# Token attention of a decoder: Q and K projections as three products of split fp32r parts, weights split step by step, and the last unit of each batch summed by VectorE alone

## The reference, cut to what matters

```python
def _attn_block(q_src, k_src, v_src, Wq, Wk, Wv, Wo, bo):
    q = _split_heads(q_src @ Wq)
    k = _split_heads(k_src @ Wk)
    v = _split_heads(v_src @ Wv)
    dots = jnp.einsum('bhid,bhjd->bhij', q, k) * SCALE
    attn = jax.nn.softmax(dots, axis=-1)
    out = jnp.einsum('bhij,bhjd->bhid', attn, v)
    ...
    return out @ Wo + bo
out = x1 + _attn_block(x1, x2, x2, Wq, Wk, Wv, Wo, bo)
return _attn_block(out, out, x1, Wq, Wk, Wv, Wo, bo)
```

## Time and profile before

| what | value |
|---|---|
| median of 3 runs | 2540.93 us (2538.76 to 2542.99) |
| the profiled execution's own time | 2538.74 us, its span 2537.0 us |
| a unit in the middle of stage c | 22.4 to 22.6 us |
| mean granted TensorE clock | 0.955 of 2.4 GHz |
| busy over the span | PE 91%, DVE 58%, ACT 43%, POOL 43% |
| stage b | about 502 to 721 us |
| stage c | about 721 to 1644 us: batch 0 to 1151, batch 1 after it |

### The profile page before, as it was taken

How to read it: one execution, slowest core, us unless ns; L and a number is a source line. 1 busy time by engine, 2 the same in 40 slices (tenths; PEclk the granted TensorE clock), 3 DMA queues, 4 the chain that set the end, 5 groups by cost and what they waited for, 6 DMA issues and landing times.

```text
span 2537.0 us, 34125 instructions
## 1 busy us (share of the span) xinstructions
PE 2317.5 (91%) x12790; PEld 1410.6 (56%) x12790; DVE 1466.7 (58%) x2191; ACT 1089.5 (43%) x2285; POOL 1091.9 (43%) x795
## 2 busy tenths in 40 slices
PE   6989999879988999998999998699899589979998
PEld 3333443357744444444544443488656466768887
DVE  6778678357735666662666663342443656655556
ACT  1667567623323444441344444042321457743223
POOL 2556546424443788875577888133400122100000
PEclk7899989989999999999999999799999799989999
DMA  6445333222110111011001111056210051010001
GB/s 128 119 89 96 76 57 71 68 79 37 1 1 1 14 14 14 10 14 5 5 10 14 14 14 14 7 133 173 32 73 18 34 131 56 1 50 26 1 1 34
DMA packets 136594, 110.29 MB, mean 43 GB/s; under 512 B 74759, under 2 KB 114165, under 8 KB 136429
## 3 DMA queue, kind: packets, MB, share of 16 engines
q1 hardware_dynamic: 99277, 107.16, 15.8%
q0 software_dynamic: 36864, 0.15, 4.2%
q10 hardware_dynamic: 288, 0.79, 0.2%
HBM read 83.11 MB, written 12.35 MB: 38 GB/s over the span
## 4 chain that ended last, share of the span: by engine, by line
PE 78%; DVE 10%; ACT 4%; POOL 2%; DMA 2%; issue 2%; SPq 2%; ACTq 0%; DVEq 0%; POOLq 0%
PE PS L115 74%; SPq L141 2%; POOL c_AC L119 2%; DVE g_SS L119 1%; PE PS L1181 1%; ACT a_P L834 1%; DVE a_MX L728 1%; PE PS L347 1%; DVE g_st L1266 1%; DMA a_KS<-a_KL 1%; PE PS L348 1%; DVE c_MX L1707 1%; DVE X L391 0%; ACT g_SS L1338 0%; POOL adj L340 0%
## 5 line engine op out<-in xcount | busy, mean ns | idle before, releaser
L340 POOL DMA_INDIRECT adj<-e_EE,e_IX x256 | 412.8, 1612 | 459.3 <-DMA adj<-e_EE,e_IX 344.6
L119 POOL TENSOR_TENSOR c_AC<-c_AC,c_P 128x1024 f32<-128x1024 f32 x160 | 401.3, 2508 | 98.9 <-DVE c_AC L119 91.4
L1707 DVE TENSOR_REDUCE c_MX<-PS 128x2 f32<-128x1024 f32 x256 | 312.8, 1222 | 193.6 <-PE PS L115 192.6
L1793 ACT ACTIVATE c_P<-PS 128x1024 f32<-128x1024 f32 x256 | 249.8, 1023 | 226.2 <-PE PS L115 218.1
L728 DVE TENSOR_REDUCE a_MX<-PS 128x2 f32<-128x1024 f32 x256 | 303.5, 1220 | 58.0 <-PE PS L115 56.4
L834 ACT ACTIVATE a_P<-PS 128x512 f32<-128x512 f32 x512 | 270.7, 602 | 89.5 <-PE PS L115 84.9
L115 PE MATMUL PS<-c_P,c_VV 128*64 128x512 f32 x1024 | 249.2, 608 | 0.0
L124 POOL TENSOR_SCALAR e_EQ<-e_KR,e_KC 128x128 bf16<-128x128 f32 x256 | 162.4, 634 | 160.3 <-DMA e_KR<-adj_key 122.1
L115 PE MATMUL PS<-a_QS,a_KS 64*128 64x512 f32 x512 | 195.5, 464 | 20.7 <-ACT a_P L834 8.6
L115 PE MATMUL PS<-a_KS,a_QS 48*128 48x512 f32 x512 | 171.7, 476 | 10.3 <-DVE a_MX L728 5.0
L115 PEld LDWEIGHTS PS<-a_QS,a_KS 64*128 64x128 f32 x512 | 84.5, 190 | 173.6 <-ACT a_P L834 96.3
(11 more groups left out here) (491 smaller groups left out, 4506.5 us busy)
## 6 DMA issues: line engine op xcount, KB each, us to landing
e_KR<-adj_key SPq DMA_DIRECT2D x64, 256.0 KB, 3.4
f_W<-in_L_ffn_w SPq DMA_DIRECT2D x16, 1024.0 KB, 6.3
c_RB<-c_r SPq DMA_DIRECT2D x60, 128.0 KB
g_FB<-in_fside_1x16xSxS SPq DMA_DIRECT2D x8, 616.0 KB, 8.0
a_QS<-a_QH SPq DMA_DIRECT2D x32, 128.0 KB
adj<-e_zt SPq DMA_DIRECT2D x16, 256.0 KB, 4.3
adj<-e_EE,e_IX POOLq DMA_INDIRECT x256, 3.1
d_AJ<-adj SPq DMA_DIRECT2D x8, 512.0 KB, 5.1
```

What stands on the lines that cost most here:

```text
L119: return v.e.tensor_tensor(o, a, b, op)
L340: g.e.indirect_dma_start(self.adj, bass.IndirectOffsetOnAxis(ap=self.IXE[:, k:k + 1], axis=0), self.EE[:, k:k + 1], None, compute_op=ALU.a ...
L1707: v.e.reduce_max(MX[:, w % 2, :, qt, kh], bank(0, 2).rearrange("p (h n) -> p h n", h=2), AX, negate=True).then_inc(*smax_dve.up())
L1793: s.e.activation(PB[t % NP][:, :, :].rearrange("p h n -> p (h n)"), bank(2 + 2 * (t % 2), 2), ACT.Exp, scale=0.125).then_inc(*st_act.up())
```

## The change

1. At the end of stage b each tile is split as it is turned: ACT writes the coarse fp32r part over XT (c_XH), DVE writes the rest (c_XF). The rest of batch 0 lies over b_WO, that of batch 1 over c_OT, from where it goes to DRAM (c_fine); `xt` jobs begin at step 6 instead of 3, since b_WO is in use until then. b_YY has 8 buffers.
2. The weights of a pair are split into c_WS just before their use: `coarse` (two ACT casts of 128x128) and `fine` (two DVE subtractions of 128x128, both inputs in SBUF), once for Wk and once for Wq. In units with odd w up to 27, except 15, they stand at n = 3 to 6. Pairs 0, 1 and 9 are split ahead of the loops.
3. A projection is six fp32r matmuls. In pair 0 the two Q projections use bank 6.
4. In units 15 and 31 DVE does all seven `add`, and POOL does no `acc`.
5. Three 1 MB loads in stage c (`fetch`): the rest of batch 1 for pair 8 (at w = 13, n = 6) and for the later pairs, and Wo again (w = 15, n = 6).
6. `out` of a batch's first four tiles waits for 15 scaled units of it, not 16.

```diff
+    def over(self, name, first, skip, shape, dt=F32R):
+
+        return self.nc.alloc_sbuf_tensor_at(name, shape, dt, offset=self.places[first] + skip)
 
 
 def mm(pe, o, l, r, first=True, last=True):
...
@@ -1056,6 +1061,8 @@
                 for q in range(4):
                     yield "u", 0, q
             if first:
+                if 6 <= i < 9:
+                    yield "xt", 2 * i - 12
                 if 1 <= i < 17:
                     yield "turn", i - 1
                 if i < 16:
@@ -1076,8 +1083,9 @@
                     yield "root", (i - 5) // 4
                 if 5 < i < 20 and i % 4 == 2:
                     yield "norm", (i - 6) // 4
-            if i >= lag:
-                yield "xt", i - lag
+
+            if i >= (6 if first else lag):
+                yield "xt", 2 * i - 11 if first and i < 9 else i - lag
 
     jobs = list(schedule())
     nth = numbered(jobs)
...
                     ins = v.e.bn_aggr(st8[:, i % 8, 6:8], st8[:, i % 8, 0:6])
                     if i % 4 == 3:
                         ins.then_inc(*var_dve.up())
+            elif kind == "xt" and first:
+                i, = a
+                cols = slice(128 * i, 128 * i + 128)
+                v.wait_ge(xt_act, i + 1)
+                v.wait_ge(u_pe, 8)
+                tt(v, K.fine[i // 8][:, :, 128 * (i % 8):128 * (i % 8) + 128], halves(bank(7)[:, 0:256]),
+                   K.coarse[:, :, cols].bitcast(F32), ALU.subtract).then_inc(*xl_dve.up())
             elif kind == "norm":
                 q, = a
                 four = slice(4 * (q % 2), 4 * (q % 2) + 4)
...
             elif kind == "xt":
                 i, = a
                 s.wait_ge(xt_pe, i + 1)
-                s.e.copy(XT[:, :, i * 128:i * 128 + 128], halves(bank(7)[:, 0:256])).then_inc(*xt_act.up())
+                s.e.copy((K.coarse if first else XT)[:, :, i * 128:i * 128 + 128],
+                         halves(bank(7)[:, 0:256])).then_inc(*xt_act.up())
             elif kind == "root":
                 q, = a
...
@@ -1404,7 +1420,10 @@
                     dma(sp, UO[0:80, b, 9, :], udram[b, 1152:1232, :]).then_inc(*u_in[b].up())
                     if not (first or b):
                         bias(*range(2, 8))
-        if not first:
+        if first:
+            sp.wait_ge(xl_dve, 16)
+            dma(sp, K.fdram, K.fine[1][:, :, :]).then_inc(*K.fine_out.up())
+        else:
             K.experts.load_router(sp, A)
             for e in range(2):
                 K.experts.load(sp, A, e)
...
     MT = sb(c, "c_MT", [8, 2, 128], F32R)
+
+    split_w = K.over("c_WS", "LS", 0, [128, 2, 2, 2, 128])
+    WS = [[split_w[:, w, part, :, :] for part in range(2)] for w in range(2)]
+    XH = [K.coarse[:, k, :] for k in range(2)]
+
+
+    WOF, WVF = K.fine[0][:, :, :], K.over("c_WVF", "b_WV", 0, [128, 2, 1024])[:, :, :]
     mdram = K.nc.dram_tensor("c_m", [2, 8, 128], F32R, kind="Internal").ap()
     sdram = K.nc.dram_tensor("c_s", [2, 512], F32, kind="Internal").ap()
     rdram = K.nc.dram_tensor("c_r", [128, 8], F32, kind="Internal").ap()
...
@@ -1461,7 +1488,17 @@
 
         return w % 16 == 15
 
+    def lead(w):
+
+        return 7 if direct(w) else 2
+
+    def leads(w):
+        return sum(map(lead, range(w)))
+
     def schedule():
+        for w in (1, 0):
+            yield "coarse", 0, w
+            yield "fine", 0, w
         yield "prep_k", 0, 0
         yield "prep_q", 0
         yield "prep_k", 0, 1
@@ -1478,6 +1515,11 @@
                     yield "s", 0, kt
                     if kt >= 4:
                         yield "s", 1, kt - 4
+            for w in (1, 0):
+                yield "coarse", 8 * b + 1, w
+                yield "fine", 8 * b + 1, w
+            if b:
+                yield "fetch", 2
             if b == 0:
                 yield "row", 0
                 yield "m", 0
...
                         yield "m", w + 1
-                    if n in (3, 4):
+                    if 3 <= n < lead(w) + 3:
                         yield "add", w, n - 3
-                    if n > 3:
+                    if n - 1 > lead(w):
                         yield "acc", w, n - 1
                     if n == 0 and not first:
                         yield "acc", w - 1, 7
@@ -1507,6 +1549,10 @@
                         yield "recip", w - 2
                     if n == 4 and not first and w - 2 >= 16 * b:
                         yield "scale", w - 2
+                    if w % 2 and w % 16 != 15 and w // 2 + 2 < 16 and 2 < n < 7:
+                        yield ("coarse", "fine")[(n - 3) % 2], w // 2 + 2, n < 5
+                    if n == 6 and w in (13, 15):
+                        yield "fetch", w // 14
                     if n % 2 == 0:
                         continue
...
@@ -1532,7 +1578,8 @@
                     if n in (1, 3, 5):
                         yield "send", 1
             w = 16 * b + 15
-            yield "acc", w, 7
+            yield "add", w, 5
+            yield "add", w, 6
             yield "pv", w, 6
             yield "turn_ou", w
             yield "recip", w - 1
@@ -1565,7 +1612,7 @@
     def added(t):
 
         w, n = divmod(t, 8)
-        return (acc_dve, 2 * w + max(n, 1)) if n < 3 else (acc_pool, 5 * w + n - 2)
+        return (acc_dve, leads(w) + max(n, 1)) if n <= lead(w) else (acc_pool, 7 * w - leads(w) + n - lead(w))
 
     def tensor(_):
...
                 pe.wait_ge(*free[bk])
+
+        def product(w, P, bk, src):
+
+            b = P // 8
+            pe.wait_ge(ws_dve, 2 * P + 2 - w)
+            if b:
+                pe.wait_ge(fine_in, 2 if P > 8 else 1)
+            fine = WVF if P > 8 else WOF
+            high, low = WS[w]
+            parts = [(W, part, k) for k in range(2) for W, part in (
+                (high, XH[k][:, src]), (low, XH[k][:, src]), (high, fine[:, k, src.start - 1024 * b:src.stop - 1024 * b]))]
+            for q, (W, part, k) in enumerate(parts):
+                ins = mm(pe, bank(bk), W[:, k, :], part, q == 0, q == 5)
+            return ins
...
                 t, = a
                 bk = 2 + t % 4
-                pe.wait_ge(ot_pool, 16 * (t // 8 + 1))
+                pe.wait_ge(ot_pool, 16 * (t // 8) + 15 + t % 8 // 4)
+                pe.wait_ge(wo_in, 1)
                 bank_free(bk)
                 for p in range(8):
                     ins = mm(pe, bank(bk)[:, 0:256], OT[:, p, t % 8 * 128:t % 8 * 128 + 128], W0.WO[:, p, :], p == 0, p == 7)
...
             kind, *a = job
-            if kind == "prep_k":
+            if kind == "fine":
+                P, w = a
+                v.wait_ge(ws_act, 2 * P + 2 - w)
+                for k in range(2):
+                    ins = tt(v, WS[w][1][:, k, :], weight(w, P, k), WS[w][0][:, k, :].bitcast(F32), ALU.subtract)
+                ins.then_inc(*ws_dve.up())
+            elif kind == "prep_k":
                 P, half = a
                 cols = slice(half * 512, half * 512 + 512)
...
                 v.wait_ge(qh_act, w + 1)
-                tt(v, QL[w % 3][:, :], bank(7), QH[w % 3][:, :].bitcast(F32), ALU.subtract).then_inc(*ql_dve.up())
+                tt(v, QL[w % 3][:, :], bank(prep_bank(w // 2, False)), QH[w % 3][:, :].bitcast(F32), ALU.subtract).then_inc(*ql_dve.up())
             elif kind == "s":
...
                 t = 8 * w + more
                 v.wait_ge(st_act, t + 2)
                 if more:
-                    v.wait_ge(acc_dve, 2 * w + 1)
+                    v.wait_ge(acc_dve, leads(w) + more)
                 elif w > 1:
                     v.wait_ge(sum_pe, w - 1)
...
             kind, *a = job
-            if kind == "prep_k":
+            if kind == "coarse":
+                P, w = a
+                if P and w:
+                    s.wait_ge(k_pe, 2 * P)
+                elif P:
+                    s.wait_ge(q_pe, 2 * P)
+                if P % 8 == 1:
+                    s.wait_ge(v_pe, 16 * (P // 8 + 1))
+                for k in range(2):
+                    ins = s.e.copy(WS[w][0][:, k, :], weight(w, P, k))
+                ins.then_inc(*ws_act.up())
+            elif kind == "prep_k":
...
@@ -1875,6 +1964,18 @@
                     dma(sp, MR[w % 3][64 * h:64 * h + 1, :],
                         mdram[w % 2][4 * h:4 * h + 4, :].rearrange("j q -> (j q)").rearrange("(o n) -> o n", o=1)).then_inc(
                         *m_in[w % 2].up())
+            elif kind == "fetch":
+                n, = a
+                if n == 1:
+                    sp.wait_ge(q_pe, 18)
+                    dma(sp, W0.WO, A["L0_xattn_Wo"].rearrange("(c p) n -> p c n", p=128)).then_inc(*wo_in.up())
+                else:
+                    sp.wait_ge(K.fine_out, 1)
+                    if n:
+                        sp.wait_ge(v_pe, 32)
+                    else:
+                        sp.wait_ge(q_pe, 16)
+                    dma(sp, WVF if n else WOF, K.fdram).then_inc(*fine_in.up())
             elif kind == "spread":
                 w, = a
...
             ectx.close()
```

(16 more changed lines are left out.)

50 lines of the change are left out of this document (27 added, 23 removed).

## The result

The median of 5 runs is 2517.56 us (2515.36 to 2521.82), against 2538.76 us (2534.32 to 2542.99) for the kernel before on the same chip: a ratio of 0.9921, 95% interval 0.9906 to 0.9936. That is 21 us faster; forecast were 36.6 us. The time is inside the range of 2484 to 2524 us and outside the narrower one, 2495 to 2512, that the forecast had for its own mechanism. The profiled execution has a span of 2515.8 us, 21.2 less than the 2537.0 of before.

The account below looks back on a forecast made before the run. PE was taken to bound stage b and mid stage c, with waits on POOL at batch ends. Terms -33.0 - 3.0 - 3.1 - 13.6 + 0.5 + 15.6 = -36.6 us gave 2502.1 us profiled, 2504 median, range 2484 to 2524.

Parts of the forecast that it names:

- Projections in the loops: Stage c loops: 60 projections fall from 1.92 to 1.37 us of PE each, 33.0 us saved (bounds 24 to 33).
- Collisions: Odd units: the second weight-subtraction pair waits for POOL's acc, PE loses 1.2 us in 13 units, +15.6 us.
- if collisions fell elsewhere than at n = 6: Odd units: one of the signs that the prediction is wrong; no size given.
- End of batch 0: Last unit of batch 0: DVE's adds let sum start earlier, 3.1 us saved (bounds 4.3 and 0).
- End of batch 1: Unit 31: sum no longer waits for POOL, output starts at 1581.0 instead of 1594.62, 13.6 us saved (10 to 15).
- Start: Start of stage c: alternating banks hide drains, less later first projection and pair 1 split, 3.0 us saved (0 to 4.2).
- Stage b: Stage b: one DVE subtraction per tile is covered by PE and costs nothing; 6.7 us without the cover.
- loads: Stage c: small DMAs of the c_s chain queue behind the 1 MB loads, +0.5 us (bounds 0 and +6).
- POOL becomes the bound: Rival, loops: both pairs always hold POOL 0.58 us, costing 6 us in 27 units, 2495 us; chance 0.05.
- the first pair is split too: Rival, odd units: POOL gets between the subtractions, PE loses 2.0 us in 13 units, 2514 us; chance 0.15.
- slower: Rival, odd units: DVE held at n = 4 and 6, clock down, 7.5 us each, 2586 us; chance 0.05.
- the tail that isn't gained: Rival, unit 31: DVE's seven adds wait, sum is no earlier, 12 us missing, 2516 us; chance 0.05.

Follow-up runs that it names:

- e12: Kernel before with its fp32 projections, plus e9's end-of-batch adds and moved reciprocal: 2517.19 us, ratio 0.9912.
- e9: e7 with five DVE adds in unit 30 and its reciprocal between the last two adds of unit 31: 2499.08 us, ratio 0.9844.
- e8: e7 with the projection products emitted behind the four pv instead of ahead of them: 2537.46 us, ratio 0.9992.
- e1: Changed kernel without 13 of the 16 weight splits, later projections reusing weights of pairs 1 and 9 (output wrong): 2504.54 us, ratio 0.9867.
- e3: Changed kernel with the subtraction pairs earlier in odd units, behind the first and second add: 2510.74 us, ratio 0.9888.
- e7: Changed kernel with the early places of e3, and in unit 17 both subtraction pairs at n = 3: 2506.49 us, ratio 0.9870.
- e4: Changed kernel with units 15 and 31 adding as before (two on DVE, five on POOL), split output wait kept: 2530.13 us, ratio 0.9970.
- e5: Kernel before with only DVE's adds in units 15 and 31, its sum wait and the split output wait: 2521.48 us, ratio 0.9927.
- e10: e7 with casts and subtractions of pair 0 ahead of the last tile of stage b: 2507.42 us, ratio 0.9873.
- e2: Changed kernel without the coarse-weight by fine-input product, four matmuls a projection instead of six (output wrong): 2498.11 us, ratio 0.9845.
- e6: Changed kernel with both subtraction pairs in a row behind the second add (n = 4): 2522.57 us, ratio 0.9951.

## Why the prediction came out as it did

**Projections in the loops (-33.0).** This step failed by size. The row of the last stage has matmuls of one form in a row; here each product stands between others, 64*128 and 128*64, and pays 0.1 us at both ends. It saves 1.92 - 1.59 = 0.33 us, 20 us in all by the rows, and two products shorten a unit without collisions by 0.60 us, 18 us in 60. I had named a bound on this side, 1.5 us (by its own terms 25 us saved, not 24), and taken the other end; the measured price lies beyond the bound. e12 against e9 gives 15.8 us for the products where the splits meet nothing. The Trainium skill (TensorEngine Tiling (Array Packing), Key Properties) says that a change of tiling mode drains TensorE; e8 agrees, 0.1 us with either neighbour ahead, and this rule should have moved the choice.

**Collisions (+15.6).** Right in mechanism, place and nearly in price: the first pair gets through and holds POOL for 0.1 us, the second meets `acc`; 1.08 us a unit, in 11 units, 11.9 us (unit 1, counted among the 13, lost nothing). The margin was thin: the subtraction came 0.13 us behind the `acc`. The step missed unit 17, +6 us by the two profiles: there the norms stand between add and pair. e1, e3 and e7 show both parts. I had written the prediction off if collisions fell elsewhere than at n = 6; in this one unit they did. The Trainium skill (SBUF — State Buffer, Who interferes with whom) also counts `tensor_scalar` among the operations that can take the shared ports. The trace agrees: the norm, with one tile as input, lasted 3.54 us beside an `acc` and 0.40 without. I had used the page for two-input instructions alone. The profile of before had shown it: two of its norms, at 1233.9 and 1240.2 us, lasted 1.10 and 1.50 us while an `acc` ran.

Together the two steps were to give 17.4 us in the loops. With the end of batch 0 they gave 1.8.

**End of batch 0 (-3.1).** 3.2 us between e4 and the changed kernel. On the kernel before the same edit is worth 1.4 (e5). Both numbers have the clock in them. Counted from the c_MM of unit 16, the first V product began at 22.7 us before and in e4, at 19.6 in the changed kernel and at 20.6 in e5: the edit moves it by 3.1 and 2.1 us. From there to the next transposition the same work took 4.6 to 6.2 us over the fourteen profiles, 4.79 in before, 6.00 in after. The stretches of before, then of e4:

```profile
1156.99:1161.78 4.79, 4.79 (x9) 1.99 (x9) 0.00 (x0) 0.96 (x2) 2.82 (x3) 0.72 0.09 0
```

```profile
1152.82:1158.98 6.16, 6.16 (x10) 2.51 (x10) 0.00 (x0) 0.96 (x2) 4.00 (x3) 0.56 0.07 1
```

So that e4 stands 1.1 us above before in this stretch is 1.4 us of lower clock, behind the same waits of PE (6.2 and 2.8 us), and not a wait that the change brought.

**End of batch 1 (-13.6).** 14.4, and 14.0 when made alone. The chain of unit 30 was late next, as said. Its c_RB left SP 30.0 us behind the last c_MM (31.3 by the forecast: the 30.1 of before and 1.25), and landed in 3.4 us (1567.83 to 1571.27) in place of 2.92.

**Start (-3.0).** The two profiles give 0.3. The first product came 2.2 us later behind the last exponential (19.63 against 17.45), 1.7 forecast; the first V 1.2 us sooner (30.23 against 31.41), 4.2 forecast. The term left out is the clock: from the first product to the first V took 10.60 us, and 8.57 in e10, where the clock stayed at 1.00 there (8.1 forecast), so 2.0 of the missing 3 us are its. The splits of pair 1 cost 0.8 us ahead of the first c_MM (5.00 us behind the last V product, 4.19 before), 1.2 forecast. PE ran at 0.51 of 2.4 GHz, which is its lower level of 1.2 GHz, over the first products, and had run at 1.00 there before:

```profile
717.00:723.00 6.00, 4.92 (x12) 3.89 (x13) 1.59 (x5) 1.29 (x5) 3.90 (x5) 0.51 0.50 178
```

With this stretch at 74.1, 77.6 and 75.9 us in the three profiles of before's start, and 73.2 to 74.8 in eleven of the new one, the means differ by 1.7 us; from the first V product to the last the two longer ones (e5, e12) took 41.9 and 40.2 us where before took 38.5, with a granted clock of 0.68 over 4 us in e5. One pair of profiles can't tell more.

**Stage b (0) and loads (+0.5).** Stage b is full as before. The loads were not tried alone; no wait of PE names them.

**The rivals.** "POOL becomes the bound" was priced at 6 us and did not come, but only since the collisions kept PE slow: e1 and e2 reach it. The rival "the first pair is split too" did not happen; e6 made it happen. The "slower" mechanism, DVE held twice and the clock down, 7.5 us, occurred in one unit of 13, at 6 us and with the norm as a third wait. By their number alone the split pair (2514 us) and the tail that isn't gained (2516 us) came nearest to the measured 2517.6; neither happened.

**Why the total was nearer than its terms.** 13 to 15 us of the products' saving did not exist and 3 of the start, and unit 17 took 6; the collisions were 4 us cheaper, and 5.5 us came from ahead of stage c, which by the table is spread: that part was luck. The medians differ by 21 us as well, 3 more than the stretches in which I can show a gain (1.7, 1.8 and 14.4 us); that is within the interval, and not explained.

## What to carry to other kernels

Price a matmul where it will stand: time from its start to the start of the next kind, with neighbours of another tile form, not from a run of its own kind; here that was 0.2 us in 1.6. A short instruction on an engine that shares a port costs nothing or what is left of the other's instruction (1.06 to 2.4 us here), and a tenth of a microsecond decides it, so put it where the other engine sends or waits (e3, e7), and look at every unit that has extra work in between. When a span moves, split it at landmarks first: two of the five stretches here spread by 11 and 8 us over versions that hardly differ in them.
